# Local attention: row roots as exp(-0.5 ln) on ScalarE, q addition on GpSimd, mixed values copied by DMA, mask as four quarter products

## The reference, cut to what matters

```
qkv = h @ wqkv ; q, k, v split, 8 heads
q = l2norm(q) * qs ; k = l2norm(k) * ks          # l2norm: t / clip(|t|, 1e-12)
q, k = rotary_xpos(q, k)                          # q*cos*scale + rotate_half(q)*sin*scale
sim = 8 * q @ k.T over the own and the previous window of 64 keys
sim = where(i < j or i > j + 64 or no window, -max, sim)
o = softmax(sim) @ v ; x = x + o @ wo
```

## Time and profile before

| | |
|---|---|
| median of 3 runs | 1201.88 us |
| lowest and highest | 1197.44, 1202.96 us |
| profiled execution, its own span | 1198.7 us |
| PE, DVE, ACT, POOL busy | 93%, 86%, 77%, 73% |
| mean granted clock of TensorE | 0.972 |
| last chain, by engine | PE 63%, DVE 13%, ACT 9%, issue 9%, POOL 6% |

### The profile page before, as it was taken

One profiled execution on the slowest core, in us unless ns is written; L12 is line 12 of the kernel. 1 busy time (PEld: TensorE's weight loads), 2 busy tenths in 40 slices (PEclk: granted clock), 3 DMA queues, 4 the chain that ended last, 5 costly groups with the idle time before them and its releaser, 6 DMA issues.

```text
span 1198.7 us, 33223 instructions
## 1 busy us (share of the span) xinstructions
PE 1112.7 (93%) x11284; PEld 925.2 (77%) x11284; DVE 1026.3 (86%) x2403; ACT 926.7 (77%) x2487; POOL 874.7 (73%) x1152
## 2 busy tenths in 40 slices
PE   6899967999999989978999999989989997999996
PEld 3777754888888879966888888778867776799996
DVE  4899968999999957878999999858879997499988
ACT  4789856999999975548999999965668887777772
POOL 4799938999999963448999999934489994344431
PEclk9999987999999989989999999999989999899999
DMA  6000000000000002100010100001100000000000
GB/s 191 23 2 1 2 15 10 11 11 10 10 11 17 3 8 60 37 20 8 11 25 21 57 9 16 2 16 29 22 1 2 2 2 1 3 15 14 15 12 18
DMA packets 57287, 22.25 MB, mean 19 GB/s; under 512 B 45173, under 2 KB 55585, under 8 KB 57122
## 3 DMA queue, kind: packets, MB, share of 16 engines
q1 hardware_dynamic: 54354, 18.62, 6.3%
q10 hardware_dynamic: 2768, 1.51, 0.4%
HBM read 9.64 MB, written 2.10 MB: 10 GB/s over the span
## 4 chain that ended last, share of the span: by engine, by line
PE 63%; DVE 13%; ACT 9%; issue 9%; POOL 6%; DMA 0%; DVEq 0%; ACTq 0%; POOLq 0%
PE m_ps_y L1488 7%; PE a_ps_b L1016 5%; PE a_ps_s L924 5%; PE a_ps_t L1027 5%; PE a_ps_a L951 4%; PE a_ps_t L991 4%; PE a_ps_qk L908 4%; DVE x_e L687 3%; PE f_ps_y L1275 3%; PE f_ps_g L1286 3%; PE a_ps_s L963 2%; PE f_ps_a L1293 2%; PE a_ps_qk L909 2%; PE a_ps_qk L910 2%; PE m_ps_h L1475 2%
## 5 line engine op out<-in xcount | busy, mean ns | idle before, releaser
L1079 ACT ACTIVATE a_e<-a_ps_s,a_stat 128x128 f32<-128x128 f32 x512 | 226.6, 477 | 3.7 <-DVE a_stat L1148 3.7
L1214 POOL TENSOR_TENSOR a_stat<-a_stat,small 128x16 f32<-128x16 f32 x64 | 186.8, 2919 | 5.3
L1204 POOL TENSOR_TENSOR a_e<-a_e,a_stat 128x1024 f32<-128x1024 f32 x64 | 121.1, 1893 | 8.5 <-DVE a_stat L1127 8.5
L1079 ACT ACTIVATION_READ_ACCUMULATOR a_e<-a_ps_s,a_stat 128x1 f32 x512 | 115.8, 226 | 0.0
L1322 ACT ACTIVATE f_gl<-f_ps_g,vec 128x128 f32<-128x128 f32 (+1 forms) x192 | 55.8, 361 | 58.1 <-PE f_ps_g L1286 58.1
L1222 POOL TENSOR_TENSOR a_rot<-a_rot,a_stat 128x512 f32<-128x512 f32 x64 | 90.0, 1407 | 5.0
L1144 DVE TENSOR_REDUCE a_stat<-a_ps_s 128x8 f32<-128x1024 f32 x64 | 78.3, 1223 | 13.8 <-PE a_ps_s L924 9.0
L736 DVE TENSOR_REDUCE x_stat<-x_ps_s 128x16 f32<-128x1024 f32 x64 | 77.1, 1205 | 11.9 <-PE x_ps_s L542 11.7
L1102 DVE TENSOR_TENSOR a_rot<-a_ps_qk,a_rtab 128x512 f32<-128x512 f32 x128 | 87.1, 681 | 0.0
L1100 DVE TENSOR_TENSOR a_rot<-a_ps_qk,a_rtab 128x512 f32<-128x512 f32 x128 | 87.1, 681 | 0.0
L1216 POOL TENSOR_TENSOR a_rot<-a_rot 128x512 f32<-128x512 f32 x64 | 82.7, 1293 | 3.6 <-DVE a_rot L1102 3.5
(11 more groups left out here) (203 smaller groups left out, 3705.0 us busy)
## 6 DMA issues: line engine op xcount, KB each, us to landing
a_h<-y SPq DMA_DIRECT2D x64, 32.0 KB
f_h<-y SPq DMA_DIRECT2D x64, 32.0 KB
out_dram<-x SPq DMA_DIRECT2D x32, 64.0 KB, 1.5
a_h<-y SPq DMA_DIRECT2D x64, 31.8 KB
f_h<-y SPq DMA_DIRECT2D x64, 31.8 KB
w<-in_L_ffn_w_dram SPq DMA_DIRECT2D x2, 768.0 KB, 5.6
x<-in_x_dram SPq DMA_DIRECT2D x1, 768.0 KB, 5.7
wqkv<-in_L_ffn_wqkv_dram SPq DMA_DIRECT2D x1, 768.0 KB, 5.8
```

Source lines behind the costliest of these rows:

```text
L1079: act.activation(self.e[n % 2][:, P * i:P * i + P], ps_s[:, P * i:P * i + P], ACT.Exp, bias=stat[:, 24 + i:25 + i], scale=stat[:, root:roo ...
L1204: p.tensor_tensor(e3, e3, self.stat[n % UNROLL][:, 16:24].unsqueeze(2).broadcast_to([P, 8, P]), ALU.mult)\
L1214: p.tensor_tensor(t[:, 48:64], t[:, 32:48], g.neg_half.broadcast_to([P, 16]), ALU.pow).then_inc(self.s_n, 1)
```

## The change

- **Roots.** POOL's L1211 and L1214 go. DVE bounds the sums of squares on both sides behind L1137 (a new operation on 128x16 numbers, from SBUF to SBUF, which waits for L1137). ACT takes the logarithm of the 16 numbers ahead of q's squares and exp(-0.5 x) behind them. A factor 2^16 within the logarithm is made up for by 2^8 in the rotary tables. The table of functions that has both is loaded ahead of time, once after the tanh of the gates and once at the start of layer 1.
- **q's addition** (L1186) goes from DVE to POOL, one step later, as the first operation of POOL's step.
- **vx** is no longer written by ACT from PSUM: SP issues a DMA from `vt` to `vx`, 64 rows of 2 KB for each tile, behind the loads of h.
- **Mask.** The two products over the whole array with 512 columns each become four over its quarters (64x64), with 512 columns each, from a table that holds each half's mask for all rows.

```diff
@@ scalar, local
-            act.activation(self.vx[b % 2][rows, :], ps_b[rows, :], ACT.Copy).then_inc(self.s_vx[u], 1)
             act.activation(self.vt[n % UNROLL][:, :], ps_b[:, :], ACT.Copy).then_inc(self.s_vc, 1)
+        n = s - 2
+            if l and n == 0:
+                act.preload_act_table_set("natural_log_exp_and_others")
+            act.wait_ge(self.s_ss, 2 * k + 2)
+            act.activation(t[:, 32:48], t[:, 32:48], ACT.Ln, scale=2.0 ** ROOT_SHIFT).then_inc(self.s_rt, 1)
         n = s - 1   (squares of q)
+        n = s - 2
+            act.wait_ge(self.s_rt, 2 * k + 1)
+            act.activation(t[:, 48:64], t[:, 32:48], ACT.Exp, scale=-0.5).then_inc(self.s_rt, 1)
@@ vector, local
-            v.reduce_sum(self.stat[n % UNROLL][:, 32:48], self.sq[:, :]...).then_inc(self.s_ss, 1)
+            v.reduce_sum(norms, self.sq[:, :]...).then_inc(self.s_ss, 1)
+            v.wait_ge(self.s_ss, 2 * k + 1)
+            v.tensor_scalar(norms, norms, 1e-24, NORM_CAP, ALU.max, ALU.min).then_inc(self.s_ss, 1)
-            v.wait_ge(self.s_r, 4 * k + 2)
-            v.tensor_tensor(r, r, self.rot2[:, 0:INNER], ALU.add).then_inc(self.s_nq, 1)
@@ gpsimd, local
+        n = s - 2   (first in the step)
+            p.wait_ge(self.s_r, 4 * k + 2)
+            p.tensor_tensor(r, r, self.rot2[:, 0:INNER], ALU.add).then_inc(self.s_nq, 1)
-            p.tensor_scalar(t[:, 32:48], t[:, 32:48], 1e-24, None, ALU.max).then_inc(self.s_n, 1)
-            p.tensor_tensor(t[:, 48:64], t[:, 32:48], g.neg_half.broadcast_to([P, 16]), ALU.pow).then_inc(self.s_n, 1)
@@ sync, local
+        n = s - 4
+            sp.wait_ge(self.s_vc, k + 1)
+            after(sp, self.s_o, k - 2 - u)
+            sp.dma_start(self.vx[b % 2][rows, :], self.vt[n % UNROLL][rows, :]).then_inc(self.s_vx[2 * (b % 2) + u], 16)
@@ tensor, local
-                pe.matmul(ps_s[:, 512 * e:512 * e + 512], g.ident16, g.lmask[:, u, :]..., start=True, stop=False)
+                for x in range(2):
+                    quarter = slice(LD * e, LD * e + LD)
+                    pe.matmul(ps_s[WIN * x:WIN * x + WIN, 512 * e:512 * e + 512], g.ident16[quarter, quarter],
+                              g.lmask[quarter, u, x, :]..., start=True, stop=False)
```

More of the change, by code:

```diff
@@ L28 @@
 QK_SCALE = 8
+ROOT_SHIFT = 16
+NORM_CAP = 2.0 ** 48
 HID = 341
@@ L86, in constants @@
                 bad = np.ones((P, WIN), bool) if rel is None else (rel > 0) | (rel < -WIN)
-                m[:, u, slot] = np.where((x == w % 2)[:, None], np.where(bad, LOCAL_AWAY, 0), m[:, u, slot])
+                m[:, u, w % 2, slot] = np.where(bad, LOCAL_AWAY, 0)
     c16 = np.concatenate([np.eye(P, dtype=f), m.reshape(P, -1)], 1)
@@ L860, in __init__ @@
             self.s_oc, self.s_y, self.s_yc, self.s_qk, self.s_v, self.s_sq, self.s_r, self.s_ss, self.s_n, self.s_hr, \
-            self.s_wh, self.s_wr, self.s_nq, self.s_qc, self.s_mx, self.s_e, self.s_ec = (g.sem(f"a_{i}") for i in (
+            self.s_wh, self.s_wr, self.s_nq, self.s_qc, self.s_mx, self.s_e, self.s_ec, self.s_rt = (g.sem(f"a_{i}") for i in (
                 "tab", "z", "h", "hc", "vc", "t", "kc", "s", "en", "et", "o", "oc", "y", "yc", "qk", "v", "sq", "r", "ss", "n",
-                "hr", "wh", "wr", "nq", "qc", "mx", "e", "ec"))
-        self.s_d, self.s_vx = [g.sem(f"a_d{i}") for i in range(UNROLL)], [g.sem(f"a_vx{i}") for i in range(2)]
+                "hr", "wh", "wr", "nq", "qc", "mx", "e", "ec", "rt"))
+        self.s_d, self.s_vx = [g.sem(f"a_d{i}") for i in range(UNROLL)], [g.sem(f"a_vx{i}") for i in range(4)]
         nt = UPS * 2 * LD
@@ L898, in sync @@
             load_shifted(sp, self.h, self.s_d, self.g.y, n, k)
+        n = s - 4
+        if 0 <= n < T:
+            k, u, b = T * l + n, n % 2, n // 2
+            rows = slice(0, WIN) if u else slice(WIN, P)
+            sp.wait_ge(self.s_vc, k + 1)
+            after(sp, self.s_o, k - 2 - u)
+            sp.dma_start(self.vx[b % 2][rows, :], self.vt[n % UNROLL][rows, :]).then_inc(self.s_vx[2 * (b % 2) + u], 16)
         if s == 16 and l:
@@ L1055, in scalar @@
             act.wait_ge(self.s_qk, 2 * k + 1)
-            after(act, self.s_ss, k)
+            after(act, self.s_ss, 2 * k - 1)
             act.activation(self.sq[:, 0:INNER], ps_qk[:, 0:INNER], ACT.Square).then_inc(self.s_sq, 1)
+        n = s - 2
+        if 0 <= n < T:
+            k, t = T * l + n, self.stat[n % UNROLL]
+            act.wait_ge(self.s_rt, 2 * k + 1)
+            act.activation(t[:, 48:64], t[:, 32:48], ACT.Exp, scale=-0.5).then_inc(self.s_rt, 1)
         n = s - 3
@@ L1135, in vector @@
             v.wait_ge(self.s_sq, 2 * k + 2)
-            after(v, self.s_n, 4 * (k - 4) + 2)
-            v.reduce_sum(self.stat[n % UNROLL][:, 32:48], self.sq[:, :].rearrange("p (h d) -> p h d", d=LD), axis=AX_X)\
-                .then_inc(self.s_ss, 1)
+            after(v, self.s_rt, 2 * (k - 4) + 2)
+            norms = self.stat[n % UNROLL][:, 32:48]
+            v.reduce_sum(norms, self.sq[:, :].rearrange("p (h d) -> p h d", d=LD), axis=AX_X).then_inc(self.s_ss, 1)
+            v.wait_ge(self.s_ss, 2 * k + 1)
+            v.tensor_scalar(norms, norms, 1e-24, NORM_CAP, ALU.max, ALU.min).then_inc(self.s_ss, 1)
         n = s - 4
@@ L1160, in vector @@
             after(v, self.s_t, k - 1)
-            after(v, self.s_n, 4 * (k - 1) + 3)
+            after(v, self.s_n, 2 * (k - 1) + 1)
             self.rotate(v, ps_qk, n, k, 1)
@@ L1613, in build @@
                             "a": [(local.s_ec, k), (local.s_qc, k), (local.s_kc, k)],
-                            "y": [(local.s_yc, k), (local.s_oc, k), (local.s_vc, k)] + [(s, k // 2) for s in local.s_vx]}
+                            "y": [(local.s_yc, k), (local.s_oc, k), (local.s_vc, k)]}
         local.taken[1] = {"qk": [(mlp.s_gl, 3 * T)], "a": [(mlp.s_hc, T)], "b": [(mlp.s_hc, T)], "t": [(mlp.s_ac, 3 * T)],
```

43 lines of the change are left out of this document (21 added, 22 removed).

## The result

The changed kernel takes 1244.5 us (median, 1241.1 to 1249.6), against 1202.2 us of the kernel before on the same chip: a ratio of 1.037, 95% interval 1.034 to 1.040. It is slower, and the forecast of 1247 us held to 0.2%. The profiled execution has a span of 1241.3 us, 42.6 more than before.

A forecast was written before the change was run, and what follows sets the result against it. PE was taken to pace the kernel before, 7.87 us a step. The profiled 1198.7 + 50.4 (56 steps x 0.90) - 6 (ramps) + 0.5 (table load) = 1243.6; the runs' median lies 3.2 higher, so 1247 us, range 1205 to 1264.

The forecast's parts named there:

- The step that decides: Bounding of the norms on DVE, L1163: ready 0.45 us into POOL's normalization, kept out to its end, 312.76 instead of 311.47.
- The ring: Chain of waits through DVE and POOL from L1163's end to its next end: a step of 8.77 us, 0.90 more.
- The ramps: Start of each layer, first three steps: bound, power and roots shorten; 0 to 12 us gained over both layers, 6 taken.
- The mask: PE's mask products: four quarters run side by side, 0.21 us less a step, which vanishes in PE's wait.
- q's addition to POOL: DVE loses 0.6 to 0.7 us of work, POOL gains 1.29 us; the addition holds up the normalization behind it.
- Roots on ACT: Two operations on 16 numbers where ACT waits for PE: cost 0, upper end 0.3 us a step.
- vx by DMA: vx leaves after `vt` is written and is needed two steps, some 15 us, later: cost 0.
- Where PE waits: Sign in nearly all local steps: PE's L919 waits for L1125, about 1 us each.
- no lockout: Rival: L1163 is too small to be kept out, or normalization out of its way; PE paces, 7.66 us, 1184; chance 0.18.
- Alternating steps: Rival: L1163 is blocked every other step; steps of 7.66 and 8.74 us alternate, mean 8.20, 1214 us; chance 0.13.
- The tables don't thrash: Denies a rival on ACT: logarithm and exponential in different sets, two 1.28 us loads a step, 1327 us; chance 0.01.

## Why the prediction was right

- **The step that decides**, L1163 locked out: right in mechanism and size. It is ready 0.45 to 0.48 us into the normalization (predicted 0.45) and ends 0.02 to 0.04 behind it, in every regular step. This is shown by taking it away, by changing its form, by cutting the normalization in two and by moving what stands ahead of it.
- **The ring**: 8.74 us between the ends of L1163 at 330.38 and 339.12 (predicted 8.77), by its parts, each from start to start: 1.24 to L1180, 1.20 to L1125, 0.76 to k's addition, 1.38 to the product, 1.00, 1.24, 1.92. The mean over 28 steps is 8.73 and 8.70, since each layer starts with two uneven ones (7.46 and 9.21, 6.97 and 9.20). The two layers cost 47.0 us instead of 50.4, the largest error in the sum.
- **The ramps**: -5.4 and, behind the layers, +1.0, together -4.4, where -6 + 0.5 was taken. So two errors, -3.4 and +1.1, cancel in part. The power's 2.92 us are gone, and the table load of layer 1 no longer stands ahead of an exponential; what each of these gave was not tried.
- **The mask**: 0.21 us a step was taken. L935 follows L976 after 0.24 us where L924 followed L963 after 0.53, so it was 0.29, and the change of PE's step (7.87 to 7.58) is as large. The four records of L976 take 0.41 us together, so they do run side by side. In the changed kernel the gain vanished, as predicted.
- **q's addition to POOL**: its own price was right (1.28 us on POOL), and the product fell to 1.04 (L1242). The prediction said of the longer products only that they began beside q's addition on DVE; it is the same lockout from the other side.
- **Roots on ACT**: they cost nothing, but not as told. ACT does wait in L1069, 1.87 us a step, 110 us in all, for L1163. It is hidden, since the exponentials need L1173 as well, which is as late: it ends at 340.46, and the first exponential starts at 340.50. The bounding behind the maxima shows the price of a later logarithm, a ring of 7.97 us.
- **vx by DMA**: 0, and 0 measured, in the kernel without L1163 (1175.1 against 1174.8 us).
- **Where PE waits**: wrong in place. I named L919 behind L1125, 1 us each. It waits in L1040 behind L1180, 0.79, and then only 0.18 in L919: the transposes of the exponentials, ahead of L919, use the buffer that DVE's late copy of q's transposes still reads. The sum per step, 0.97, is nearly the same.
- **The rivals**: no lockout (1184) is refuted here, but its arithmetic was near what the kernel without L1163 does, 1175. Alternating steps were not seen. The tables don't thrash: there are 7 loads in the trace, none in the regular steps.
- **What the rows did not carry**: the earlier trace rows show no wait worth the name. The cast L1549 took 0.18 us there, and its median over 32 tiles is 0.16. And the rule as the prediction tells it is on copy, cast and tensor_scalar, while L1148 in the earlier trace rows is a tensor_tensor with two inputs in SBUF. What stood for L1163 was thus above all, a larger tensor_scalar. That 16 numbers are held up as well was shown only by the changed kernel.
- **What I did not see**: that the ring alone was not the whole price. By the prediction's ring the bounding without q's addition on POOL would cost next to nothing (7.51 us). It costs 32 us in the kernel before. The forecast did not hang on it, but my expectation for q's addition on DVE did, and failed by 18 us.

Open: one step of layer 0 takes 9.12 us (277.46 to 286.58) instead of 8.74. DVE's L1180 starts 0.45 us behind L1173 there and not 0.08, and the profile puts 0.28 of that to issue, a wait for nothing that it shows. The kernels with whole mask products, with the normalization in two and with the floor in the logarithm and q's addition on DVE have the same gap; no run was made for it.

## What to carry to other kernels

A small elementwise operation on DVE, SBUF to SBUF, can cost what is left of the GpSimd instruction that it meets, and not its own length (not every pair does, see below). Look for it as a busy operation that ends together with one on POOL, for here it never showed as a wait. Before adding one, ask whether its work fits into an instruction that exists (here a bias) or a form that isn't held up (here a reduction), and put the longest GpSimd instruction where DVE only reduces or reads PSUM. Then look for the ring: what stands ahead of that GpSimd instruction in its queue belongs to the price.

## What the runs showed of the hardware

- A reduction of 32 numbers to 16 ran in 0.19 us inside POOL's normalization; a tensor_scalar on 16 numbers at the same place took 1.46 and ended with the normalization.
- Which engine pays went by who started first, and a delay elsewhere flipped it: q's addition 0.69 and POOL's product 1.45 us before, 1.12 and 1.04 with one DVE instruction more.
- Not every POOL instruction keeps DVE out: beside the power L1214, 2.92 us long, DVE's L1148 ran in 0.17. Why the power is different was not tried. A DVE operation on one number was not held up either, in the kernel before:

```profile
1024.81 0.43 POOL L1585 TENSOR_SCALAR m_rt<-c,m_rt 128x8 f32<-128x8 f32 x1
...
1025.08 0.15 DVE L1563 TENSOR_SCALAR m_rt<-m_rt 128x1 f32<-128x1 f32 x1
```

- Two halves of the normalization take 2.04 us and let DVE in between them.
